# Rounding the second token group in place, its last view at the turn from self to cross tiles, and other lists for the front

## The chip, the cores and the metric

The program runs on one core of one Trainium2 chip, in one launch. The metric is the device time of that launch in microseconds (us). A profiled execution also gives the start and length of each instruction on each engine: PE (TensorE), DVE (VectorE), ACT (ScalarE), POOL (GpSimd) and SP, which here only issues DMAs.

## What is computed

A block of two decoder layers over 1024 tokens of 256 channels (16 batches of 64 tokens, `ctx_2048` having the same shape). The reference, cut to what matters here:

```python
x = x + tanh(g_xattn[0]) * L0_attention(layernorm(x), mask, ctx, ctx, Wq, bq, Wk, bk, Wv, bv)
x = x + tanh(g_ffn[0])   * L0_ffn(layernorm(x))       # ternary weights, 8-bit tokens
x = x + tanh(g_xattn[1]) * L1_attention(layernorm(x), ctx)
x = x + tanh(g_ffn[1])   * L1_experts(layernorm(x))   # shared + 7 routed, top 3

def L0_ffn(x):                       # bit_linear rounds x to 8 bits and w to -1, 0, 1
    h = silu(bit_linear(x, w_gate)) * bit_linear(x, w_up)
    return bit_linear(rms_norm(h, ln_weight), w_down)

def L1_attention(hidden, cond):      # 16 query heads, 8 key heads of 128
    ln_out = ln(hidden) * ln_w + ln_b
    q, k, v = (fp8(ln_out / in_scale[m]) * in_scale[m] @ w[m].T * w_scale[m] for m in "qkv")
    core = gqa(ln(q), ln(k), v)                        # self part
    qx = fp8(ln_out / qx_in_scale) ...                 # fourth view of ln_out
    kx, vx = split(cond @ w_kv_x.T)
    xout = gqa(ln(qx), ln(kx), vx)                     # cross part
    return fp8(concat(core, xout) / smooth) @ wproj.T * scale
```

So the normed tokens are rounded to fp8 four times, once for each "view" (q, k, v, qx), each with its own input scale.

## The kernel before, in words

**Two programs one behind the other.** `front` computes the first layer (attention and the ternary feed-forward layer), the products of the context with `w_kv_x` (24 of 32 units, `context(e)`) and the splitting of the first weights of the second layer into a high and a low part. `grouped_attention` computes the second layer: 16 tiles of 128 tokens, of which tiles 0 to 7 are the self part and tiles 8 to 15 the cross part, and behind them the experts.

**Order.** Each engine has a list of calls that is written out by hand; an engine takes its calls strictly in that order, and semaphores make a call wait for others. SP's list sets the order of the loads. The tokens are worked on in two groups s = 0, 1 of four 128-row pieces. In `front` the calls that matter here are: `weights.mean / centre / high / low (n)`, the mean over heads on DVE, its subtraction on POOL (L185), the high part on ACT (L195) and the low part on DVE (L202) of weight block n; `context_mean / centre_context`, the same for the context weights; `tern.column_sum / scale / clip`, the rounding of the three ternary weights on ACT (L580, L594) and DVE (L600, L602); `gate_up`, `gated`, `hidden(s, n)` (L1280, L1057, L863), the products, the SiLU and the 16 products of the two halves of the gated layer; `square`, `weigh`, `hidden_largest`, `hidden_scales`, `round_hidden` (L889), the norm and 8-bit rounding of `f_h`; `turn_hidden` (L1294), `keep_hidden` (L1072) and `down` (L1306), its transposes and the last product; `turn_normed`, `weigh_tokens` (L1332, L1085), the normed tokens of the second layer.

**The fp8 rounding.** It has a division by the scale on ACT (`over_scale`, L2039 for the second token group) and five instructions on DVE: clip, exponent bits, power, add, subtract (L1797 to L1809). Group 0 of the tokens is rounded in `front` by `round_two`. Group 1 is tokens 512 to 1023, which tiles 4 to 7 (views 0 to 2) and 12 to 15 (view 3) use; it is rounded in `grouped_attention`, in `late_tokens(view)`, through the buffers `yb` and `kb` with two halves each. So `over_scale` of view v waits for `late_tokens(v - 2)`, and `unload(0, ...)`, which writes `yb` next, waits for all four. The calls stand in DVE's list so: `late_tokens(0)` and `(1)` in `ahead(0)`, `(2)` and `(3)` at the start of `both_own(0)`, ahead of `less_max(0, 0)` (L1742, L1746), the maximum that scores and exponents of tile 0 go through.

**Tiles.** `both_own(n)` works on tile n's attention and on the projections of tile n + 1; `both_cross(n)` does the same from n = 7 on, where tile n + 1 is a cross tile. `copy_tile(n)` on POOL (L1607) takes a tile's views out of `xq`; `fp8(n, h)` on POOL (L1632, `g_cat`) is the last step of the rounding of a tile's attention; `own_out.low` (L231) the low part of the output weights.

## Time and profile before

| | before |
|---|---|
| median of 3 runs | 638.5 us (638.17 to 638.55) |
| profiled execution, its own time | 637.83 us |
| its span, first to last instruction | 636.1 us |
| mean granted clock of PE | 0.976 of full speed |
| busy share of the span, from the page | PE 92%, DVE 78%, ACT 58%, POOL 58% |
| `front`, to about | 145.1 us |
| first scores of tile 0 turned into exponents | 183.8 us |
| end of the self tiles, about | 331 us |

The profiled execution is 1.7 us longer than its span and 0.7 us shorter than the median. An engine's busy share says little by itself; what matters in each stretch is which engine is never idle, and what the others wait for.

### The profile page before, as it was taken

Reading aid. Unit: us, or ns where it says so; the run is one execution under the profiler, and the core shown is the slowest. Engines: PE = TensorE matmul, PEld = TensorE weight load, DVE = VectorE, ACT = ScalarE, POOL = GpSimd, SP = SyncE. Lnnn points to the kernel's source line nnn. Section 1 sums busy time; section 2 is a strip of 40 time slices with the busy share of each in tenths; the row PEclk is TensorE's granted clock in tenths of the full one; section 3 lists DMA queues with packets and bytes.
Section 4 is the critical chain, followed back from the end, with each engine's and each line's share of the span. In section 5 each row is a group of like instructions: output and inputs, shape, how many; then the busy total and the mean of one; then the engine's idle time right before and its main releaser. Section 6 shows DMA issues by size and latency. Waiting matters only on the chain.

```text
span 636.1 us, 10615 instructions
## 1 busy us (share of the span) xinstructions
PE 582.5 (92%) x3738; PEld 471.0 (74%) x3738; DVE 496.7 (78%) x924; ACT 370.2 (58%) x669; POOL 366.1 (58%) x299
## 2 busy tenths in 40 slices
PE   3999786978869999999998999999999999999996
PEld 1655333644558898888987898888889888888886
DVE  4488999886998999998979889999987956333333
ACT  1477675485666676776767765676666235434231
POOL 3100765303656878778778866766766733855431
PEclk9999898998969999999999999999999999999999
DMA  7981220114413112131085132322110100311001
GB/s 236 294 305 66 84 82 33 68 66 152 144 39 133 36 60 73 35 124 43 2 312 174 46 116 67 85 83 80 49 57 18 34 1 2 112 39 33 2 1 66
DMA packets 44564, 54.86 MB, mean 86 GB/s; under 512 B 8417, under 2 KB 30817, under 8 KB 44513
## 3 DMA queue, kind: packets, MB, share of 16 engines
q1 hardware_dynamic: 44512, 54.20, 26.1%
q8 instruction: 30, 0.49, 0.3%
q14 instruction: 22, 0.17, 0.1%
HBM read 41.60 MB, written 12.58 MB: 85 GB/s over the span
## 4 chain that ended last, share of the span: by engine, by line
PE 62%; DVE 5%; POOL 4%; ACT 3%; issue 2%; DMA 1%; DVEq 0%; POOLq 0%; ACTq 0%
PE g_proj L2220 12%; PE g_proj L2306 7%; PE g_scores L2261 6%; PE g_turn L2250 6%; PE g_op L2287 5%; PE g_op L474 2%; PE g_op L476 2%; PE g_op L475 2%; PE g_proj L459 2%; PE g_proj L461 2%; PE g_proj L460 2%; PE g_turn L2270 2%; POOL g_rs L1613 1%; PE g_turn L459 1%; PE g_scores L459 1%
## 5 line engine op out<-in xcount | busy, mean ns | idle before, releaser
L1613 POOL TENSOR_TENSOR g_rs<-g_ve,neg_half 128x4 f32<-128x4 f32 x80 | 83.5, 1048 | 37.8 <-DVE g_ve L1723 37.4
L1632 POOL TENSOR_TENSOR g_cat<-g_yb,g_kb 128x1024 fp32r<-128x1024 bf16 x32 | 71.0, 2226 | 41.1 <-DVE g_yb L1780 41.1
L2220 PE MATMUL g_proj<-w_hi,g_xqc 128*128 128x512 f32 x192 | 85.1, 443 | 1.5 <-DVE g_qn L1736 1.2
L2220 PE MATMUL g_proj<-w_lo,g_xqc 128*128 128x512 f32 x192 | 77.2, 402 | 0.0
L503 POOL TENSOR_TENSOR m_h_lo<-m_h,m_h_hi 128x512 fp32r<-128x512 f32 x32 | 41.4, 1296 | 57.1 <-ACT m_h_hi L490 57.1
L1723 DVE TENSOR_REDUCE g_ve<-g_sq 128x4 f32<-128x516 f32 x80 | 54.6, 684 | 18.4 <-ACT g_sq L1980 16.8
L2261 PEld LDWEIGHTS g_scores<-g_qkT 128*128 128x128 f32 x512 | 62.4, 196 | 8.1 <-issue 6.9
L2261 PE MATMUL g_scores<-g_qkT 128*128 128x64 f32 x512 | 62.8, 277 | 4.8 <-DVE g_ex L1746 4.8
L2250 PE MATMUL g_turn<-ident,g_qn 128*128 128x128 f32 x384 | 58.0, 278 | 1.3 <-DVE g_qn L1736 1.3
L1980 ACT ACTIVATE g_sq<-g_proj 128x512 f32<-128x512 f32 x80 | 47.7, 596 | 16.3 <-PE g_proj L2220 14.5
L2250 PEld LDWEIGHTS g_turn<-ident,g_qn 128*128 128x128 f32 x384 | 45.0, 143 | 10.8 <-DVE g_qn L1736 2.6
L1323 PE MATMUL f_bank<-f_w_ctx,f_ctxT 128*128 128x512 f32 x96 | 47.1, 622 | 1.8 <-ACT f_kept L1079 1.1
L490 ACT ACTIVATE m_h_hi<-m_h 128x512 fp32r<-128x512 f32 x32 | 20.2, 632 | 48.6 <-DVE m_h L497 48.6
L2220 PEld LDWEIGHTS g_proj<-w_hi,g_xqc 128*128 128x128 f32 x192 | 37.3, 194 | 10.2 <-DVE g_qn L1736 2.1
L2014 ACT ACTIVATE g_qkT<-g_turn,c_lnp 128x512 f32<-128x512 f32 x48 | 36.5, 777 | 14.2 <-PE g_turn L2250 14.2
L1736 DVE TENSOR_TENSOR g_qn<-g_proj,g_rs 128x512 f32<-128x512 f32 x64 | 43.7, 682 | 1.3 <-POOL g_rs L1613 1.3
L2287 PE MATMUL g_op<-g_pT,g_v 64*128 64x128 f32 x512 | 37.2, 285 | 5.5 <-ACT g_pT L2033 5.5
L513 DVE SCALAR_TENSOR_TENSOR x_res<-g_op,m_we,x_res 128x256 f32<-128x256 f32 x64 | 27.8, 478 | 17.8 <-PE g_op L476 17.8
L2287 PEld LDWEIGHTS g_op<-g_pT,g_v 64*128 64x128 f32 x512 | 31.1, 187 | 14.4 <-ACT g_pT L2033 10.0
L2220 PEld LDWEIGHTS g_proj<-w_lo,g_xqc 128*128 128x128 f32 x192 | 37.4, 195 | 5.5 <-issue 0.8
L555 POOL TENSOR_TENSOR ln_rstd<-ln_ve,neg_half 128x4 f32<-128x4 f32 x6 | 6.6, 1094 | 58.3 <-DVE ln_ve L542 58.3
L2014 ACT ACTIVATE g_qkT<-g_turn,x_lnp 128x512 f32<-128x512 f32 x48 | 36.2, 771 | 5.6 <-PE g_turn L2250 5.6
(247 smaller groups left out, 1662.4 us busy)
## 6 DMA issues: line engine op xcount, KB each, us to landing
kvx_rows<-f_kept SPq DMA_DIRECT2D x24, 256.0 KB, 2.4
g_ksq<-kvx_rows SPq DMA_DIRECT2D x8, 512.0 KB, 4.4
g_kraw<-kvx_rows SPq DMA_DIRECT2D x16, 256.0 KB, 3.2
g_v<-kvx_rows SPq DMA_DIRECT2D x8, 512.0 KB, 4.0
m_raw<-in_L_W SPq DMA_DIRECT2D x16, 256.0 KB, 3.0
c_raw<-in_L_wqT SPq DMA_DIRECT2D x4, 512.0 KB, 5.8
f_w_ctx<-in_L_wkvxT SPq DMA_DIRECT2D x4, 512.0 KB, 8.1
c_praw<-in_L_wprojT SPq DMA_DIRECT2D x4, 512.0 KB, 5.4
```

The lines of the kernel that those rows point to most:

```text
L1323: last = T.matmul(context_bank(e)[:], ctxT[:, c_, tile * P:(tile + 1) * P], w_ctx[:, chunk, c_, :], start=c_ == 0, stop=c_ == KT - 1)
L1613: G.tensor_tensor(rs[:, at % NORMS, :], ve[:, at % NORMS, :], k["half"][:, 0:4], ALU.pow).then_inc(q["rs_done"], 1)
L1632: G.tensor_tensor(cat[:, h].rearrange("p h (b s) -> p b h s", b=2), yb[:, h, :].rearrange("p (b h s) -> p b h s", b=2, s=SEQ), kb[:, h, :] ...
L1723: V.tensor_reduce(ve[:, at % NORMS, :], sq[:, at % 2], AX.X, ALU.add).then_inc(q["ve_done"], 1)
L1736: V.tensor_tensor(qn[:, i % 2, :].rearrange("p (h d) -> p h d", d=D), bank(n, i)[:].rearrange("p (h d) -> p h d", d=D), bcast(rs[:, at % N ...
L1980: A.activation(sq[:, at % 2, :, 0:D], bank(n, i)[:].rearrange("p (h d) -> p h d", d=D), ACT.Square, scale=D ** -0.5).then_inc(q["sq_done"], 1)
L2014: A.activation(qkT[:, n % 2, at:at + 4, :], turns[TURN_BANK[i]][:].rearrange("p (h m) -> p h m", h=4), ACT.Identity, bias=lnp[:, w + 1:w + ...
L2220: last = T.matmul(bank(n, i)[:], xqc[:, n % 2, view * KT + c_, :], w[:, c_, :], start=c_ == 0 and part == 0, stop=c_ == KT - 1 and part == 1)
L2250: last = T.transpose(out, qn[:, i % 2, h * D:(h + 1) * D], k["ident"][:])
L2261: last = T.matmul(sp_[:, (g * 2 + b) * SEQ:(g * 2 + b + 1) * SEQ], qkT[:, n % 2, 2 * kv + b, :], qkT[:, n % 2, HEADS + kv, rows], start=Tr ...
L2287: last = T.matmul(op[:, b, g * P:(g + 1) * P], v[rows, n % 2, kv * D:(kv + 1) * D], pT[rows, h, g, :], start=True, stop=True)
L2306: last = T.matmul(proj[OUT_BANK][:, 0:E], cat[:, h, hd % (2 * GH), :], w[hd // 4][:, hd % 4, :], start=hd == 0 and part == 0, stop=hd == H ...
```

## The change

Four things are done.

1. **In place.** `over_scale` writes the divided tokens straight to `xq`, for every view, and waits for no rounding. `late_tokens` rounds them there (`round_tokens`, which `early_tokens` shares), with `kb[:, 0]` alone as its second buffer. The five instructions of a view are the same.
2. **Where the views are rounded.** `late_tokens(2)` stands behind `less_max(0, 0)` and the two `sums` of tile 1; `late_tokens(3)` stands in `both_cross(7)`, behind `less_max(7, 0)`, and waits there for `fp8(6, 0)` on POOL (`cat_done`).
3. **Waits.** `copy_tile(4)` waits for three views, `copy_tile(12)` for the fourth; `unload(0, ...)` waits for none; `fp8(0, ...)` waits for the last `over_scale`.
4. **Other lists in `front`**, on all five engines. No call is added or removed; the one reciprocal `inv` and all others only move.

The diff, cut to its core (of the lists, the first lines on SP; what the others do is shown in the orders below):

```diff
@@ SP, front @@
             sp.dma_start(k['x'][:, 0:ST, :], source[:, 0:ST, :]).then_inc(x_loaded[0], 16)
-            sp.dma_start(k['x'][:, ST:TILES, :], source[:, ST:TILES, :]).then_inc(x_loaded[1], 16)
+            weights.load(sp, t, 0)
+            weights.load(sp, t, 1)
+            sp.dma_start(mask[:], t['mask'].rearrange('(n p) s -> p n s', p=P)).then_inc(q['v_loaded'], 16)
...
+            weights.load(sp, t, 2)
+            sp.dma_start(k['x'][:, ST:TILES, :], source[:, ST:TILES, :]).then_inc(x_loaded[1], 16)
@@ POOL, grouped_attention @@
                     if n == ST:
-                        pool.wait_ge(q["late_done"], 4)
+                        pool.wait_ge(q["late_done"], 3)
...
+                    if n == TILES + ST:
+                        pool.wait_ge(q["late_done"], 4)
@@ DVE, grouped_attention @@
                 def unload(n, h):
                     dve.wait_ge(q["pv_done"], n * 2 + h + 1)
-                    if n == 0:
-                        dve.wait_ge(q["late_done"], 4)
...
+                def round_tokens(view, group, name):
+                    y, power_ = k["xq"][:, view, :, group * ST * P:(group + 1) * ST * P], kb[:, 0, :].rearrange("p (c n) -> p c n", c=KT)
+                    done = view + 1 if group else 1
+                    V.tensor_scalar(y, y, FP8_MAX, -FP8_MAX, ALU.min, ALU.max).then_inc(q[name + "_clipped"], 1)
+                    dve.wait_ge(q[name + "_clipped"], done)
+                    V.tensor_scalar(power_.bitcast(U16), y.bitcast(U16), 0x7F80, None, ALU.bitwise_and).then_inc(q[name + "_abs"], 1)
+                    dve.wait_ge(q[name + "_abs"], done)
+                    V.tensor_scalar(power_, power_, FP8_NORMAL, FP8_LIFT, ALU.max, ALU.mult).then_inc(q[name + "_power"], 1)
+                    dve.wait_ge(q[name + "_power"], done)
+                    V.tensor_tensor(y, y, power_, ALU.add).then_inc(q[name + "_big"], 1)
+                    dve.wait_ge(q[name + "_big"], done)
+                    V.tensor_tensor(y, y, power_, ALU.subtract).then_inc(q[name + "_done"], 1)
...
+                def late_tokens(view, n=0):
+                    if n > 0:
+                        dve.wait_ge(q["cat_done"], 2 * n - 1)
                     dve.wait_ge(q["over_done"], KT * (view + 1))
...
                 def both_own(n):
                     m = n + 1
-                    if n == 0:
-                        late_tokens(2)
-                    if n == 0:
-                        late_tokens(3)
                     less_max(n, 0)
                     sums(m, 0)
                     sums(m, 1)
+                    if n == 0:
+                        late_tokens(2)
                     total(n, 0)
...
                     less_max(n, 0)
+                    if n == TILES - 1:
+                        late_tokens(3, n)
                     sums(m, 1)
@@ ACT, grouped_attention @@
                 def over_scale(u):
                     view = u // KT
-                    if view > 1:
-                        act.wait_ge(q["late_done"], view - 1)
-                    A.activation(yb[:, view % 2, u % KT * CH:(u % KT + 1) * CH], k["late"][:, u % KT, :], ACT.Copy, scale=k["inv"][:, u:u + 1]).then_inc(q["over_done"], 1)
+                    A.activation(k["xq"][:, view, u % KT, ST * P:TOK], k["late"][:, u % KT, :], ACT.Copy, scale=k["inv"][:, u:u + 1]).then_inc(q["over_done"], 1)
```

**ACT in `front`, from the exponents of group 1 to the first SiLU.** Before (`f_probs` is `exponent`, `f_pT` `keep_probs`, `f_raw` `tern.scale`, `w_hi` `weights.high`, `f_kept` `keep_context`, `f_xqT` `keep_integers`, `f_silu` `gated`):

```order
L594 ACTIVATE f_raw_85<-f_raw_85,magic,tern_inverse 128x2048
L1037 ACTIVATE f_probs<-f_s 64x4x64 x2
L1041 ACTIVATE f_pT<-f_bank 128x512
L594 ACTIVATE f_raw_86<-f_raw_86,magic,tern_inverse 128x2048
L1079 ACTIVATE f_kept<-f_bank 128x512 x2
L1048 ACTIVATE f_xqT<-f_bank,unmagic 128x512 x2
L1079 ACTIVATE f_kept<-f_bank 128x512
L1057 ACT_TABLE_LOAD
L1057 ACTIVATE f_silu<-f_bank,f_dg 128x512
```

and now:

```order
L1037 ACTIVATE f_probs<-f_s 64x4x64 x2
L1041 ACTIVATE f_pT<-f_bank 128x512
L594 ACTIVATE f_raw_85<-f_raw_85,magic,tern_inverse 128x2048
L195 ACTIVATE w_hi<-c_raw_50,c_sc 128x512 x2
L1079 ACTIVATE f_kept<-f_bank 128x512
L594 ACTIVATE f_raw_86<-f_raw_86,magic,tern_inverse 128x2048
L1079 ACTIVATE f_kept<-f_bank 128x512
L1048 ACTIVATE f_xqT<-f_bank,unmagic 128x512 x2
L1079 ACTIVATE f_kept<-f_bank 128x512 x2
L195 ACTIVATE w_hi<-c_raw_51,c_sc 128x512 x2
L1057 ACT_TABLE_LOAD
L1057 ACTIVATE f_silu<-f_bank,f_dg 128x512
```

The first `tern.scale` stood ahead of the exponents and stands behind the transposed probabilities; two `weights.high` and one `keep_context` came in ahead of the first SiLU.

**PE in `front`, from the last products of the gated layer to the first `down`.** Before (L1280 is `gate_up`, L1323 `context`, L1294 `turn_hidden`, L1306 `down`):

```order
L1323 MATMUL f_bank<-f_w_ctx,f_ctxT 128x512 x4
L1280 MATMUL f_bank<-f_values,f_xqT 128x512 x8
L1294 MATMUL f_bank<-ident,f_h 128x128 x16
L1323 MATMUL f_bank<-f_w_ctx,f_ctxT 128x512 x2
L1294 MATMUL f_bank<-ident,f_h 128x128 x8
L1306 MATMUL f_bank<-f_values,f_hT 128x256 x16
L1323 MATMUL f_bank<-f_w_ctx,f_ctxT 128x512 x2
```

and now:

```order
L1280 MATMUL f_bank<-f_values,f_xqT 128x512 x4
L1323 MATMUL f_bank<-f_w_ctx,f_ctxT 128x512 x2
L1280 MATMUL f_bank<-f_values,f_xqT 128x512 x4
L1323 MATMUL f_bank<-f_w_ctx,f_ctxT 128x512 x4
L1294 MATMUL f_bank<-ident,f_h 128x128 x8
L1323 MATMUL f_bank<-f_w_ctx,f_ctxT 128x512 x4
L1294 MATMUL f_bank<-ident,f_h 128x128 x8
L1306 MATMUL f_bank<-f_values,f_hT 128x256 x8
L1323 MATMUL f_bank<-f_w_ctx,f_ctxT 128x512 x2
```

`context(14)` and `context(15)` stood ahead of the last two `gate_up` and are behind them. The second `turn_hidden` waits now behind `context(16)` and `context(17)`, which wait for the last `hidden`. On DVE the low parts of weight blocks 2, 3 and 4 stand ahead of that last `hidden` (before: of blocks 2 and 3), and `hidden_largest(1, 0)` behind it (before: well ahead of it). Farther up in DVE's list the means of blocks 2 and 3 and the first context mean, which stood between the products of `hidden`, are ahead of `hidden(0, 0)`.

**DVE in `grouped_attention`, tile 0.** Before, the five instructions of a view's rounding stand twice behind `scale(0, 5)` (L1736), and behind the second five `less_max(0, 0)` and the rest (L1797 to L1809 are the second five, L1742 and L1746 `less_max`, L1723 `sums`, L1752 and L1756 `total`):

```order
L1797 TENSOR_SCALAR g_yb<-g_yb 128x1024
L1803 TENSOR_SCALAR g_kb<-g_yb 128x1024
L1805 TENSOR_SCALAR g_kb<-g_kb 128x1024
L1807 TENSOR_TENSOR g_yb<-g_yb,g_kb 128x1024
L1809 TENSOR_TENSOR xq_all<-g_yb,g_kb 128x2x512
L1742 TENSOR_REDUCE g_mx<-g_scores 128x8
L1746 TENSOR_TENSOR g_ex<-g_scores,g_mx 128x512
L1723 TENSOR_REDUCE g_ve<-g_sq 128x4 x2
L1752 TENSOR_REDUCE g_sm<-g_ex 128x8
L1756 RECIPROCAL g_rc<-g_sm 128x8
L202 SCALAR_TENSOR_TENSOR w_lo<-x_raw_57,x_sc,w_hi 128x512 x2
```

and now, from `scale(0, 5)` on (L1787 to L1795 are the rounding of the one view that stayed):

```order
L1740 TENSOR_TENSOR g_qn<-g_proj,g_rs 128x512
L1746 TENSOR_REDUCE g_mx<-g_scores 128x8
L1750 TENSOR_TENSOR g_ex<-g_scores,g_mx 128x512
L1727 TENSOR_REDUCE g_ve<-g_sq 128x4 x2
L1787 TENSOR_SCALAR xq_all<-xq_all 128x2x512
L1789 TENSOR_SCALAR g_kb<-xq_all 128x1024
L1791 TENSOR_SCALAR g_kb<-g_kb 128x1024
L1793 TENSOR_TENSOR xq_all<-xq_all,g_kb 128x2x512
L1795 TENSOR_TENSOR xq_all<-xq_all,g_kb 128x2x512
L1756 TENSOR_REDUCE g_sm<-g_ex 128x8
L1760 RECIPROCAL g_rc<-g_sm 128x8
L202 SCALAR_TENSOR_TENSOR w_lo<-x_raw_57,x_sc,w_hi 128x512 x2
```

`less_max(0, 0)` and two sums of tile 1 are ahead of the rounding. The other view stands where the cross tiles begin, where `sums(8, 1)` (L1727) used to follow on `less_max(7, 0)` at once:

```order
L1778 TENSOR_SCALAR g_kb<-g_kb 128x1024
L1782 TENSOR_TENSOR g_yb<-g_yb,g_kb 128x1024 x2
L1746 TENSOR_REDUCE g_mx<-g_scores 128x8
L1750 TENSOR_TENSOR g_ex<-g_scores,g_mx 128x512
L1787 TENSOR_SCALAR xq_all<-xq_all 128x2x512
L1789 TENSOR_SCALAR g_kb<-xq_all 128x1024
L1791 TENSOR_SCALAR g_kb<-g_kb 128x1024
L1793 TENSOR_TENSOR xq_all<-xq_all,g_kb 128x2x512
L1795 TENSOR_TENSOR xq_all<-xq_all,g_kb 128x2x512
L1727 TENSOR_REDUCE g_ve<-g_sq 128x4
L1756 TENSOR_REDUCE g_sm<-g_ex 128x8
L1760 RECIPROCAL g_rc<-g_sm 128x8
```

## Rows read from the trace of the kernel before

**Rows 1.** Windows: us, busy (count) by engine, granted clock, DMA share, GB/s

```profile
57.70:104.00 46.30, 38.28 (x122) 16.21 (x120) 45.47 (x59) 32.67 (x55) 27.28 (x13) 0.96 0.18 69
104.00:108.00 4.00, 0.40 (x2) 0.40 (x3) 4.00 (x5) 1.40 (x3) 1.01 (x1) 0.91 0.16 59
108.00:135.00 27.00, 26.25 (x153) 18.27 (x152) 22.58 (x51) 17.55 (x30) 7.25 (x4) 0.95 0.13 50
179.00:184.00 5.00, 0.19 (x2) 0.16 (x1) 4.93 (x5) 0.84 (x2) 2.80 (x1) 0.84 0.00 0
184.00:188.00 4.00, 3.88 (x17) 3.69 (x18) 3.47 (x7) 4.00 (x9) 3.53 (x4) 0.50 0.00 0
199.00:320.00 121.00, 120.07 (x919) 105.76 (x916) 112.33 (x185) 84.22 (x160) 92.75 (x72) 1.00 0.17 55
```

**Rows 2.** Timeline of PE in tile 0: start, length, instruction [idle before]

```profile
183.88 3.65 PE L2261 MATMUL g_scores<-g_qkT 128*128 128x64 f32 x16 [4.81 <-DVE g_ex L1746]
...
187.64 0.80 PE L2220 MATMUL g_proj<-w_hi,g_xqc 128*128 128x512 f32 x1
...
191.07 0.78 PE L2220 MATMUL g_proj<-w_hi,g_xqc 128*128 128x512 f32 x1
```

**Rows 3.** Timeline of ACT in the front

```profile
46.59 2.09 ACT L594 ACTIVATE f_raw<-f_raw,magic,tern_inverse 128x2048 f32<-128x2048 f32 x1
...
56.90 0.69 ACT L1057 ACTIVATE f_silu<-f_bank,f_dg 128x512 f32<-128x512 f32 x1
```

**Rows 4.** Timeline of DVE at the first and the thirteenth product of the gated layer

```profile
57.69 0.75 DVE L863 SCALAR_TENSOR_TENSOR f_h<-f_bank,f_du,f_silu 128x512 f32<-128x512 f32 x1 [1.77 <-ACT f_silu L1057]
...
99.42 1.41 DVE L863 SCALAR_TENSOR_TENSOR f_h<-f_bank,f_du,f_silu 128x512 f32<-128x512 f32 x2
```

**Rows 5.** Groups of DVE by shape, 57.69 to 108.2 us | busy, mean ns | idle

```profile
L202 DVE SCALAR_TENSOR_TENSOR w_lo<-c_raw,c_sc,w_hi 128x512 fp32r<-128x512 f32 x6 | 6.3, 1092 | 0.0
...
L178 DVE TENSOR_REDUCE c_sums<-c_raw 128x8 f32<-128x1024 f32 x4 | 4.8, 1206 | 0.0
...
L180 DVE TENSOR_SCALAR c_sums<-c_sums 128x8 f32<-128x8 f32 x4 | 3.9, 970 | 0.1
...
L602 DVE TENSOR_SCALAR f_values<-f_values 128x2048 bf16<-128x2048 bf16 x1 | 2.7, 2728 | 0.0
...
L879 DVE TENSOR_SCALAR f_hm<-f_hm 128x4 f32<-128x4 f32 x1 | 2.3, 2287 | 0.0
```

**Rows 6.** Timeline of DVE, end of tile 0's late rounding

```profile
174.88 0.42 DVE L1797 TENSOR_SCALAR g_yb<-g_yb 128x1024 bf16<-128x1024 bf16 x1
...
176.98 0.69 DVE L1809 TENSOR_TENSOR xq_all<-g_yb,g_kb 128x1024 bf16<-128x1024 bf16 x1
...
179.69 2.71 DVE L1809 TENSOR_TENSOR xq_all<-g_yb,g_kb 128x1024 bf16<-128x1024 bf16 x1
...
182.33 0.68 DVE L1742 TENSOR_REDUCE g_mx<-g_scores 128x8 f32<-128x512 f32 x1
```

**Rows 7.** Timeline of POOL beside it

```profile
179.06 2.80 POOL L231 TENSOR_TENSOR p_lo<-c_praw,p_hi 128x1024 fp32r<-128x1024 f32 x1 [6.11 <-ACT p_hi L227]
```

**Rows 8.** Timeline of PE from the second transpose of f_h on

```profile
107.60 1.97 PE L1294 MATMUL f_bank<-ident,f_h 128*128 128x128 f32 x8 [3.64 <-DVE f_h L889]
...
132.64 2.13 PE L1306 MATMUL f_bank<-f_values,f_hT 128*128 128x256 bf16 x16
```

**Rows 9.** Groups of PE by shape, 107.6 to 134.8 us

```profile
L1323 PE MATMUL f_bank<-f_w_ctx,f_ctxT 128*128 128x512 f32 x25 | 12.6, 622 | 0.0
...
L1294 PE MATMUL f_bank<-ident,f_h 128*128 128x128 f32 x56 | 8.2, 296 | 4.3 <-DVE f_h L889 4.3
...
L1306 PE MATMUL f_bank<-f_values,f_hT 128*128 128x256 bf16 x64 | 8.0, 273 | 0.0
```

**Rows 10.** Timeline of DVE at the change from self to cross tiles

```profile
334.94 0.69 DVE L1723 TENSOR_REDUCE g_ve<-g_sq 128x4 f32<-128x516 f32 x1 [3.33 <-ACT g_sq L1980]
```

**Rows 11.** Timeline of POOL at the same place

```profile
329.38 4.62 POOL L1632 TENSOR_TENSOR g_cat<-g_yb,g_kb 128x1024 fp32r<-128x1024 bf16 x2 [2.63 <-DVE g_yb L1780]
```

More of the change, by code:

```diff
@@ L1120, in _ @@
             keep_context(2)
+            keep_context(3)
+            weights.high(act, 2)
             gated(0, 0)
@@ L1400, in _ @@
             turn_normed(0)
[L1401 removed]
             turn_hidden(1, 2)
+            down(1, 1)
             context(21)
[L1404 removed]
+            context(22)
             turn_hidden(1, 3)
```

253 lines of the change are left out of this document (114 added, 139 removed).

## The prediction

> **What bounds the kernel now.** I read the page's busy shares first: PE 92%, DVE 78%. They are averages over three kinds of stretch, so I went to windows. From 199 to 320 us (tiles 1 to 6) PE is busy 120.07 of 121.00 us at full clock [rows 1]: whatever is gained ahead of it is carried through it, and nothing that DVE does there is on the path. In the front from 57.7 to 104 us DVE is busy 45.47 of 46.30 us and PE only 38.28, so DVE's list sets the pace; from 108 to 135 us it is PE, 26.25 of 27.00 us, behind a hole in which it worked 0.40 of 4.00 us [rows 1]. In tile 0 PE is busy 0.19 us of the 5 us from 179 to 184 while DVE is busy 4.93 of them [rows 1]: PE waits 4.81 us for `g_ex` [rows 2]. These three places, and the turn to the cross tiles, are what the change touches.
>
> **Front, the start: 3.2 us later.** Before, ACT has scaled the first ternary matrix when it keeps the transposed probabilities of group 1, and scales the second directly behind them, at 46.59 [rows 3]. Now the first stands behind those probabilities too. The second transpose of tokens (1.0 us by `turn`'s eight matmuls) now stands ahead of `project_v(0)`, so I put the probabilities 1.1 us later, at 47.7. From there ACT has 2.09 + 2.09 us of scaling [rows 3], one `weights.high` (some 1.3) and one `keep_context` (0.6) between them: 54.5 where it was 48.7. Behind it DVE clips (some 1.9), and ACT, beside that, keeps integers and contexts, one more `weights.high`, then loads the SiLU table (1.3). I come to the first SiLU at 60.2 where it is 56.90 [rows 3], and to the first `hidden` at 60.9 where it is 57.69 [rows 4]: +3.2.
>
> **Front, what DVE has done by then.** Two weight means and a context mean came ahead of `hidden(0, 0)`, into time in which DVE waits. One mean is 1.21 us and a small instruction [rows 5], 1.33 in all, so three are 4.0 us. Net, DVE is 4.0 - 3.2 = 0.8 us ahead.
>
> **Front, DVE against POOL.** The small second instruction of a mean should take 0.17 us, but over four it means 0.97; a low part is six instructions of mean 1.09 where those without POOL beside them take 0.74, and single ones take 2.73 and 2.29 us [rows 5] for some 0.7 and 0.2. They run long where a big POOL operation is under way: in tile 0 a subtract of 0.69 us takes 2.71 [rows 6] from 179.69 on, until just behind the end of POOL's 2.80 us from 179.06 [rows 7]. To the end of `hidden(1, 5)` such excess is some 11.3 us: means 3.2 (4 x 0.80), the clip 2.0, the scales 2.1 + 1.1, two more small ones 1.3 and 1.6. I walked the new lists from 60.9 on with these lengths, each such instruction held until POOL's is done, and counted 9.7, since two of POOL's centrings are out of the stretch: -1.6. Against that two low parts more (1.3 each) and one `hidden_largest` less (1.1) stand ahead of that product, +1.5. It comes at about 100.1 to 100.5 us, against 99.42 + 1.41 = 100.8 [rows 4]: no gain yet.
>
> **Front, the end: -1.8 us.** Here the order on PE decides. Before, PE waits 3.64 us for the second rounded row until 107.60 [rows 8], and works at a granted 0.91 and then 0.95 [rows 1]. Now `context(14)` and `(15)` fill that hole, behind `gate_up(1, 7)` at 101.4: transposes from 104.9, then `context(16)` to 107.4, when the last `hidden` (104.5) is long there. What remains from there to the last `down` is what remained at 107.60: seven transposes of eight, six contexts, eight `down`, one `turn_normed`. At full clock these are 6.1 + 10.3 + 7.0 + 0.9 = 24.3 us; it took 27.2 (132.64 + 2.13 = 134.77) [rows 8], with contexts at a mean of 622 ns and transposes at 296, and the eight `down` 8.0 us in all [rows 9]. About 1.5 of the 2.9 us between is the clock behind the hole, which goes if the hole goes: the last `down` at 133.0, -1.8, and the tail behind it (norm, roundings) is unchanged. The loads are in another order; the one that is moved back furthest and needed soonest is the context, which comes near the end of the queue now. No engine waited for it before, its first product moves 3 us back as well, and by 57.7 the queue is all but empty (a share of 0.18) [rows 1]: I put nothing on them.
>
> **Tile 0: -2.2 us.** One view's rounding on DVE costs 2.79 us where nothing disturbs it (174.88 to 176.98 + 0.69) [rows 6]. `less_max(0, 0)` starts at 182.33 [rows 6] behind two of them and POOL's lock; now it starts when `scale(0, 5)` is done, 174.9. So `scores(0, 1)` goes from 183.88 [rows 2] to behind `project(1, 1)`, 178.9. That is 5.0 us, but not all of it arrives. Next late is ACT, whose exponents of tile 0, a split and an output weight precede `scale(1, 0)`: 184.0, and `project(1, 2)` with it, against 187.64 [rows 2]. And next the view that stayed: it waits for `own_out.low(0)` on POOL (which ends at 181.8, as before [rows 7]) and ends at 184.6, then total, low part, `less_max(0, 1)`, and `scale(1, 1)` ends at 188.7. `project(1, 3)` starts there, against 191.07 [rows 2]: -2.4. I take 0.2 off for a low part behind POOL's normalising. PE has a granted 0.50, its lower level of 1.2 GHz, from 184 to 188 [rows 1]; that should shrink, but it lies beside DVE's chain.
>
> The Trainium skill (TensorE: Matmul & The Clock Gate, HAM oscillation) says that waits between bursts keep the engine falling back to half its clock. By that rule a wait of 3 us that remains ahead of `project(1, 2)` would leave the bursts slow, and the sum would be nearer to nothing from this tile. The trace agrees that waits and half clock lie together here (0.19 of 5 us busy, then 0.50, [rows 1]).
>
> **The view that went: +1.9 us.** Behind `less_max(7, 0)` DVE is idle for 3.33 us, until 334.94 [rows 10], and the rounding takes 2.79. It would fit, if it started at once (331.6). But its clip waits for `fp8(6, 0)`, the first of two `g_cat` operations that take 4.62 us from 329.38 [rows 11]; when that is done, POOL goes on with the second, to 334.0, and DVE's clip is of the kind that runs long under POOL. Then the five end at 336.8, and `sums(8, 1)` is 1.9 us late. DVE is full from there on (the chain of waits goes through it to 352), so it is carried. The bounds: 0, if the clip gets in ahead of POOL, and 2.8, if POOL's next work is pushed too.
>
> The Trainium skill (SBUF — State Buffer, Who interferes with whom) says that whichever of a two-port DVE instruction and a GpSimd instruction starts first holds the port pair for its whole length, and the other blocks. By it the clip loses to the second `g_cat`, +1.9; by the idle row alone it would be 0.
>
> **The sum.** -1.8 - 2.2 + 1.9 = -2.1 us. The profiled execution has 637.83 us, so 635.7; the median is 0.7 above it: **636.4 us**. About 0.2% (1.3 us) can be told from no change.
>
> **Rivals.**
> - *Slower: the late start is not caught up.* POOL's operations fall on DVE's instructions as often as before (+1.6 on my walk), and DVE waits for SiLUs between products, since ACT has its high parts there; 2.5 us more for that. Then the front is +2.3, the sum +2.0: about 640.5. It decides from a `hidden(1, 5)` later than some 102.5 us. For it: ACT is behind by 3.2 us and the three means are small. Against: ACT has slack, 32.67 of 46.30 us busy [rows 1]. Chance 0.18.
> - *Tile 0 brings nothing:* by half clock or by ACT's and POOL's queues. Then -1.8 + 1.9: 638.6. For it: PE's 0.50 [rows 1]. Against: 5 us of wait are there to take. Chance 0.15.
> - *The front's end brings nothing,* since transposes wait for `keep_hidden` and the rest balances: 638.2. Chance 0.14.
> - *The moved view is hidden* in the idle 3.33 us [rows 10]: 634.5. Chance 0.13.
>
> **How the numbers follow.** The forecast, 636.4, has 0.40; its own range is 635.0 to 637.8, from half to all of each gain. Low end: the hidden view, and a little more from tile 0, 633.6. High end 640.0, just short of the slower rival; about 0.1 lies above it and 0.07 below 633.6. Faster by over 1.3 us: 0.13, and 0.36 of the forecast's 0.40, and 0.05 of the others: 0.54. Same: 0.26. Slower: 0.20, the slower rival and a little of the next.
>
> **What would show it.** The first `hidden` near 60.9 and the last near 104.5; PE without a hole of 3 us between 101 and 110; `front` ending near 143.3. From the start of tile 0 to `project(1, 3)` 2.4 us less. At the turn, a clip (now L1787) of over 2 us and `sums(8, 1)` late. The forecast is wrong if the first SiLU is late by more than 5 us, if the last `hidden` is behind 108, or if that clip is short.

## The result, and the profile after

The change makes the kernel faster: 634.0 us (median of 14 runs, 632.95 to 637.1) against 638.2 us (14 runs, 637.53 to 639.01), a ratio of 0.9941 with a 95% interval of 0.993 to 0.9951, so 3.8 us (0.59%) less; between the two medians it is 4.2. The profiled execution has 633.74 us, its span 632.0 us, 4.1 less than before. The forecast was 636.4 with a range of 633.6 to 640.0: the measured time lies near the low end of that range, and outside of the forecast's own range of 635.0 to 637.8. One of the 11 executions of e3 below (1165.1 us), and one of the kernel before beside e9 to e11 (831.49), fell in a slower state and are left out of the ratios.

Busy shares barely move. These are the lines of the page on the engines and on the clock that the throttle granted:

```profile
PE 576.7 (91%) x3735; PEld 468.2 (74%) x3738; DVE 494.6 (78%) x924; ACT 369.1 (58%) x669; POOL 365.9 (58%) x299
...
PEclk9999999988989999999998999999999999999999
```

The windows that answer to [rows 1], each at about the place where that work stands now (columns as there):

```profile
59.10:102.00 42.90, 32.43 (x104) 13.31 (x105) 41.81 (x58) 29.09 (x49) 22.62 (x12) 1.00 0.16 62
102.00:106.00 4.00, 4.00 (x17) 2.23 (x16) 4.00 (x5) 2.48 (x6) 4.00 (x2) 1.00 0.35 131
104.00:131.00 27.00, 26.10 (x156) 17.94 (x155) 21.78 (x49) 18.77 (x32) 7.22 (x5) 1.00 0.16 59
175.00:180.00 5.00, 1.12 (x11) 0.98 (x9) 4.12 (x7) 4.46 (x10) 4.48 (x3) 1.00 0.00 2
180.00:184.00 4.00, 3.70 (x12) 2.57 (x12) 3.93 (x7) 1.08 (x2) 2.72 (x3) 0.57 0.00 0
195.00:316.00 121.00, 120.12 (x922) 105.58 (x921) 112.30 (x185) 84.35 (x161) 92.96 (x72) 1.00 0.18 60
...
333.00:337.00 4.00, 3.68 (x20) 3.68 (x21) 3.21 (x5) 2.73 (x4) 4.00 (x5) 0.63 0.21 75
```

The 4 us in which PE worked 0.40 us are full now, and the tail of the front has a granted 1.00. In tile 0 PE still waits, and still works at its lower level behind the wait. A new window at the lower level (0.63) is there at the turn to the cross tiles.

**Front.** DVE's first and last product of the gated layer, then PE from the last products of that layer on, and its last `down`:

```profile
59.09 0.75 DVE L863 SCALAR_TENSOR_TENSOR f_h<-f_bank,f_du,f_silu 128x512 f32<-128x512 f32 x1 [2.57 <-ACT f_silu L1057]
...
97.36 0.74 DVE L863 SCALAR_TENSOR_TENSOR f_h<-f_bank,f_du,f_silu 128x512 f32<-128x512 f32 x1
...
101.33 0.74 DVE L863 SCALAR_TENSOR_TENSOR f_h<-f_bank,f_du,f_silu 128x512 f32<-128x512 f32 x1
```

```profile
98.16 1.04 PE L1280 MATMUL f_bank<-f_values,f_xqT 128*128 128x512 bf16 x4
99.03 3.60 PE L1323 MATMUL f_bank<-f_w_ctx,f_ctxT 128*128 128x512 f32 x8
102.47 1.04 PE L1294 MATMUL f_bank<-ident,f_h 128*128 128x128 f32 x8
103.34 3.60 PE L1323 MATMUL f_bank<-f_w_ctx,f_ctxT 128*128 128x512 f32 x8
...
128.72 2.13 PE L1306 MATMUL f_bank<-f_values,f_hT 128*128 128x256 bf16 x16
```

Against [rows 4] the first `hidden` is 1.4 us later, `hidden(1, 5)` ends 2.7 us earlier (98.1 for 100.8), and against [rows 8] the last `down` ends at 130.85, 3.9 us earlier.

**Tile 0.** PE at the three products that the prediction follows ([rows 2]), then DVE's maximum and the view that stayed, and POOL beside it ([rows 6, 7]):

```profile
174.23 1.89 PE L2258 MATMUL g_scores<-g_qkT 128*128 128x64 f32 x16
180.19 0.63 PE L2217 MATMUL g_proj<-w_hi,g_xqc 128*128 128x512 f32 x1 [4.07 <-ACT g_qn L2005]
...
185.25 0.50 PE L2217 MATMUL g_proj<-w_hi,g_xqc 128*128 128x512 f32 x1 [1.36 <-DVE g_qn L1740]
```

```profile
171.75 0.68 DVE L1746 TENSOR_REDUCE g_mx<-g_scores 128x8 f32<-128x512 f32 x1
...
176.41 1.59 DVE L1787 TENSOR_SCALAR xq_all<-xq_all 128x1024 bf16<-128x1024 bf16 x1
...
175.36 2.36 POOL L231 TENSOR_TENSOR p_lo<-c_praw,p_hi 128x1024 fp32r<-128x1024 f32 x1 [5.54 <-ACT p_hi L227]
```

`project(1, 3)` comes at 185.25 for 191.07, 5.8 us earlier: 1.9 more than the front gave. By the second output of attention of that tile (192.05 for 198.23) it is 2.3 us.

**The turn.** DVE's view and the sums behind it, POOL beside it, and PE ([rows 10, 11]); the last two lines are PE at this place before:

```profile
325.77 2.36 DVE L1787 TENSOR_SCALAR xq_all<-xq_all 128x1024 bf16<-128x1024 bf16 x1 [0.31 <-POOL g_cat L1636]
328.16 0.43 DVE L1789 TENSOR_SCALAR g_kb<-xq_all 128x1024 uint16<-128x1024 uint16 x1
...
330.43 0.68 DVE L1727 TENSOR_REDUCE g_ve<-g_sq 128x4 f32<-128x516 f32 x1
...
331.25 1.01 POOL L1615 TENSOR_TENSOR g_rs<-g_ve,neg_half 128x4 f32<-128x4 f32 x1 [3.41 <-DVE g_ve L1727]
...
333.32 0.66 PE L2267 MATMUL g_turn<-ident,g_ex 128*128 128x128 f32 x4 [3.19 <-POOL g_ex L1625]
333.73 0.36 PE L2303 MATMUL g_proj<-p_hi,g_cat 128*128 128x256 f32 x1
...
334.08 0.41 PE L2303 MATMUL g_proj<-p_hi,g_cat 128*128 128x256 f32 x1
```

```profile
337.85 0.66 PE L2270 MATMUL g_turn<-ident,g_ex 128*128 128x128 f32 x4 [1.57 <-POOL g_ex L1623]
...
338.46 0.28 PE L2306 MATMUL g_proj<-p_lo,g_cat 128*128 128x256 f32 x1
```

The clip of 0.43 us takes 2.36, the sums come at 330.43 where 334.94 less the 6.15 us gained until then would be 328.79: 1.6 us late. PE waits 3.19 us where it waited 1.57, and then products of 0.28 us take 0.41. The granted clock of the 4 us from the end of the wait is 0.59 (333.3 to 337.3), before it was 1.00 (337.85 to 341.85).

**A table by stretches.** The executions begin this work up to 1.6 us apart, so I count from ACT's last copy of keys (L1031; 39.02 before, 38.90 after). Some loads, means and other calls ahead of it are in another order too; to that mark they make 0.12 us. Stretches in us: from there to the end of the last `down` (front); to the second output of attention on PE in tile 0; to that in tile 6; to that in tile 9 (the turn, tiles 7 to 9); and on to tile 15. Differences of start times read from PE's timeline:

| kernel | front | tile 0 | tiles 1 to 6 | turn | rest | median us | ratio to before, 95% |
|---|---|---|---|---|---|---|---|
| before | 95.75 | 63.46 | 126.17 | 58.71 | 111.12 | 638.2 | |
| the change | 91.95 | 61.20 | 126.20 | 60.74 | 111.19 | 634.01 | 0.993 to 0.9951 |
| e1_tiles_alone | 97.18 | 60.98 | 126.19 | 60.73 | 111.15 | 638.48 | 0.9998 to 1.0015 |
| e2_lists_alone | 91.97 | 63.86 | 126.21 | 59.20 | 111.10 | 634.35 | 0.9922 to 0.9949 |
| e3_view_back | 91.98 | 66.19 | 126.28 | 59.13 | 111.19 | 638.05 | 0.9981 to 0.9999 |
| e4_view_tile4 | 93.56 | 60.92 | 129.75 | 58.71 | 111.27 | 636.43 | 0.9958 to 0.9982 |
| e5_scale_early | 91.97 | 61.14 | 126.19 | 60.72 | 111.27 | 635.01 | 0.9928 to 0.9952 |
| e6_means_late | 96.15 | 61.23 | 126.25 | 60.79 | 111.11 | 640.16 | 1.001 to 1.0034 |
| e7_halves_own | 91.98 | 61.06 | 127.61 | 59.26 | 111.27 | 634.73 | 0.9928 to 0.9951 |
| e8_halves_cross | 91.94 | 61.53 | 126.30 | 69.45 | 111.22 | 642.98 | 1.005 to 1.0074 |
| e9_scales_early | 91.96 | 61.60 | 126.40 | 60.74 | 111.28 | 635.3 | 0.9936 to 0.996 |
| e10_contexts_back | 94.46 | 61.43 | 126.35 | 60.75 | 111.24 | 637.45 | 0.9974 to 1.0006 |
| e11_half_half | 91.95 | 61.05 | 127.48 | 59.58 | 111.24 | 634.31 | 0.993 to 0.9958 |
| e12_silu_first | 91.43 | 62.13 | 126.21 | 61.44 | 111.27 | 634.64 | 0.9922 to 0.9954 |

The change against before: -3.80 - 2.26 + 0.03 + 2.03 + 0.07, and -0.12 of start, are the 4.05 us between the two last outputs (490.18 and 494.23). One profiled execution stands behind each row, and single ones stray (the front of e4 has 93.56, where eight others with the same lists on DVE and PE have 91.94 to 91.98; that of e1 has 97.18 with the lists of before).

### The profile page after: what moved, and what is told of

Its sections match the earlier page's. It is cut to its first block, busy times and chain, and to the rows that moved or that the text cites. A ratio compares the mean times of both kernels' runs of the same rounds, so it can differ in the third digit from the quotient of the medians.

```text
span 632.0 us, 10614 instructions
## 1 busy us (share of the span) xinstructions
PE 576.7 (91%) x3735; PEld 468.2 (74%) x3738; DVE 494.6 (78%) x924; ACT 369.1 (58%) x669; POOL 365.9 (58%) x299
## 4 chain that ended last, share of the span: by engine, by line
PE 64%; DVE 6%; POOL 3%; issue 3%; ACT 2%; DVEq 0%; POOLq 0%; ACTq 0%
PE g_proj L2217 13%; PE g_proj L2303 8%; PE g_scores L2258 7%; PE g_turn L2247 6%; PE g_op L2284 5%; PE g_op L474 3%; PE g_op L475 2%; PE g_op L476 2%; PE g_proj L459 2%; PE g_proj L461 2%; PE g_proj L460 2%; PE g_turn L2267 2%; PE g_op L2225 1%; POOL g_rs L1615 1%; PE g_turn L459 1%
## 5 line engine op out<-in xcount | busy, mean ns | idle before, releaser
L1727 DVE TENSOR_REDUCE g_ve<-g_sq 128x4 f32<-128x516 f32 x80 | 54.8, 685 | 16.9 <-ACT g_sq L1979 14.9
L2258 PEld LDWEIGHTS g_scores<-g_qkT 128*128 128x128 f32 x512 | 60.9, 192 | 2.7 <-issue 1.4
L2258 PE MATMUL g_scores<-g_qkT 128*128 128x64 f32 x512 | 61.0, 272 | 0.0
L1323 PE MATMUL f_bank<-f_w_ctx,f_ctxT 128*128 128x512 f32 x96 | 44.0, 594 | 0.9 <-ACT f_kept L1079 0.9
```

What stands on the lines that cost most here:

```text
L1323: last = T.matmul(context_bank(e)[:], ctxT[:, c_, tile * P:(tile + 1) * P], w_ctx[:, chunk, c_, :], start=c_ == 0, stop=c_ == KT - 1)
L1727: V.tensor_reduce(ve[:, at % NORMS, :], sq[:, at % 2], AX.X, ALU.add).then_inc(q["ve_done"], 1)
L2258: last = T.matmul(sp_[:, (g * 2 + b) * SEQ:(g * 2 + b + 1) * SEQ], qkT[:, n % 2, 2 * kv + b, :], qkT[:, n % 2, HEADS + kv, rows], start=Tr ...
```

## The experiments

Kernels of e1 to e4, of e5 to e8 and of e9 to e11 ran on one chip each, e12 on a fourth. The kernel before has a median of 638.17, 638.59, 638.40 and 638.38 us on these chips, and of 638.2 where it ran beside the change; so a comparison with the change's 634.01 is uncertain by some 0.4 us on top of the spread of each kernel.

**e1: the tiles' edits without the lists.** `front` of before, `grouped_attention` of the change.

> The lists of the front as before; in-place rounding and the two moved views as in the change. Theory 1 (the gain of the whole, about 4.1 us, is the front's 3.9 and tile 0's 2.3 less the turn's 2.05, and these add up): about 0.25 us less than before, ratio 0.9996 to the kernel before, no difference that can be told, the first scores of tile 0 some 5 us earlier and the second output of attention (PE, end of tile 0) 2.3 us earlier than before. Rival (tile 0 can only give its gain when the front's end is as in the change, since half clock or the queues of ACT and POOL hold it): tile 0 gives under 1 us and the kernel is 1 to 2 us slower than before, ratio 1.002 to 1.003.

Measured 638.48, ratio 1.0007: no difference. The profile has the two parts as the theory had them: tile 0 is 2.5 us shorter (60.98 for 63.46) and the turn 2.0 longer. They cancel. The rival, that tile 0 needs the new front for its gain, falls.

**e2: the lists alone.** `front` of the change, `grouped_attention` of before.

> The kernel before with the new lists of the front alone; all views rounded in tile 0, through the buffers. Theory 1: the front ends 3.9 us earlier and all of it arrives: 3.9 us less than before, ratio 0.9939. Rival (the whole change's gain is mostly the moved views, and an earlier front is partly waited away in tile 0): under 2.5 us less, ratio above 0.996.

Measured 634.35, ratio 0.9935: all of the gain is here. The profile's front is 91.97, as with the whole change.

**e3: the fourth view back in tile 0.**

```diff
                     if n == 0:
                         late_tokens(2)
+                        late_tokens(3)
...
                     less_max(n, 0)
-                    if n == TILES - 1:
-                        late_tokens(3, n)
                     sums(m, 1)
```

> As the change, but the fourth view of the second group is rounded directly behind the third in tile 0 again, behind the first maximum and the two sums; nothing at the turn. Theory 1: the turn gives its 2.05 us back, tile 0 loses 2.3 to 2.8 (the total and the second maximum of tile 0 stand behind one more rounding of 2.8 us, and the next product of the projections waits for the scaling behind them): 0.2 to 0.8 us slower than the change. Rival (the gain of tile 0 comes from the maximum standing ahead of both roundings, and the second rounding there is free since PE waits for ACT anyway): 1.5 to 2 us faster than the change.

Measured 638.05, 4.0 us slower than the change and far outside of what both theories said. The turn gives 1.6 us back, but tile 0 loses 5.0 (66.19 for 61.20). PE in tile 0:

```profile
179.53 0.69 PE L2216 MATMUL g_proj<-w_hi,g_xqc 128*128 128x512 f32 x1 [4.07 <-ACT g_qn L2004]
...
185.02 0.66 PE L2266 MATMUL g_turn<-ident,g_ex 128*128 128x128 f32 x4 [2.67 <-POOL g_ex L1625]
187.49 0.80 PE L2216 MATMUL g_proj<-w_hi,g_xqc 128*128 128x512 f32 x1 [1.81 <-DVE g_qn L1740]
188.09 0.63 PE L2216 MATMUL g_proj<-w_lo,g_xqc 128*128 128x512 f32 x1
```

Two waits follow on the first one, and products of 0.40 us go on taking 0.63 until 192, where those of the change are back at 0.40 by 185.6. Of the 5.0 us, 3.1 are more waiting (2.67 + 1.81 against the change's 1.36), the rest is slow products. So with the maximum ahead of it, only one view has room in tile 0. At the turn, PE's wait is back at 1.56 us, and still its clock falls behind it (shown in the part on the turn below); in e4, where it doesn't, 2.0 us come back.

**e4: the fourth view in tile 4** and not at the turn, behind `total(4, 1)`, where PE is never idle.

```diff
                     total(n, 1)
+                    if n == 4:
+                        late_tokens(3, n)
                     sums(m, 3)
```

> As the change, but the fourth view is rounded in tile 4, behind the second total, where PE is the bound (120.07 of 121 us busy before) and DVE has some 1.4 us of idle time in each tile. Theory 1 (DVE is off the path there and catches up over two tiles): the turn's 2.05 us come back and nothing is lost: 2.0 us faster than the change, and no wait of PE over 0.5 us between 240 and 300 us. Rival (DVE's list feeds PE just in time, so 2.8 us less the nearest idle time are carried): PE waits about 2 us in tile 4 or 5, and the kernel is within 0.8 us of the change.

Measured 636.43, 2.4 us slower than the change. The turn gives its 2.0 us back; tiles 1 to 6 take 3.55 us more. PE behind the rounding, whose five instructions took 2.7 us undisturbed:

```profile
277.65 0.66 PE L2247 MATMUL g_turn<-ident,g_qn 128*128 128x128 f32 x4 [1.90 <-DVE g_qn L1740]
278.06 0.68 PE L2217 MATMUL g_proj<-w_hi,g_xqc 128*128 128x512 f32 x1
278.54 0.63 PE L2217 MATMUL g_proj<-w_lo,g_xqc 128*128 128x512 f32 x1
...
281.79 0.39 PE L2217 MATMUL g_proj<-w_lo,g_xqc 128*128 128x512 f32 x1
```

```profile
278.00:282.00 4.00, 4.00 (x15) 3.07 (x13) 3.80 (x7) 2.83 (x7) 3.74 (x4) 0.57 0.38 116
```

A wait of 1.90 us, and then 4 us at a granted 0.57; 3.55 less 1.90 leaves 1.65 us to the slow products. The profiled execution (637.72 us) is the slowest of the eight; that the clock falls in each of them isn't shown. The prediction's reading of that stretch as one in which nothing that DVE does is on the path was wrong: DVE feeds PE just in time there.

**e5, e9: what sets the first SiLU.** e5 moves ACT's first scaling ahead of the exponents again, e9 the second too.

```diff
+            tern.scale(act, 0)
             exponent(1)
             keep_probs(1)
-            tern.scale(act, 0)
+            tern.scale(act, 1)
             weights.high(act, 1)
             keep_context(0)
-            tern.scale(act, 1)
```

(This is e9; e5 has the first two of the four marked lines.)

> As the change, but ACT scales the first ternary matrix ahead of the exponents of group 1 again, where it is idle for 4.17 us. Theory 1 (the first SiLU is set by ACT's chain behind the transposed probabilities, and the front goes on from it): the 2.09 us come out of that chain, the first hidden comes about 2.0 us earlier (57.1), and since DVE is full from there on and PE from the end of the front, the kernel is 1.5 to 2.0 us faster than the change. Rival (the first SiLU then waits for something else, the context products or the table, or DVE's instructions meet POOL's at worse moments): under 0.5 us of gain, or a loss.

> As the change, but ACT scales both ternary matrices early: the first ahead of the exponents of group 1, the second directly behind the transposed probabilities, ahead of the high part and the first kept context. With the first alone early the first SiLU did not come earlier, since ACT then waited 2.44 us for the first context product of PE at 49.70. Theory 1 (the second scaling, 2.08 us, goes into that wait, and the chain from the first kept context to the SiLU gets shorter by it): the first SiLU about 2.0 us earlier, the last hidden and the kernel 1.5 to 2.0 us earlier than the change. Rival (PE's next products or DVE's rounding of the matrices take over): the first SiLU less than 0.7 us earlier and the time within 0.7 us of the change.

Measured 635.01 and 635.3, no better than the change. From the mark to the first `hidden` it is 20.19 us in the change, 20.19 in e5 and 20.19 in e9. Both scalings are hidden. In e9 ACT waits for PE's contexts instead:

```profile
52.58 0.60 ACT L1079 ACTIVATE f_kept<-f_bank 128x512 f32<-128x512 f32 x1 [1.12 <-PE f_bank L1323]
...
56.02 0.60 ACT L1079 ACTIVATE f_kept<-f_bank 128x512 f32<-128x512 f32 x1 [1.12 <-PE f_bank L1323]
56.51 1.32 ACT L195 ACTIVATE w_hi<-c_raw,c_sc 128x512 fp32r<-128x512 f32 x2
57.85 1.28 ACT L1057 ACT_TABLE_LOAD   x1
```

**e12: the first SiLU sooner.**

```diff
             context(2)
-            context(3)
             gate_up(0, 0)
+            context(3)
...
             keep_context(2)
-            keep_context(3)
-            weights.high(act, 2)
             gated(0, 0)
+            keep_context(3)
             tern.scale(act, 2)
             gated(0, 1)
+            weights.high(act, 2)
```

> As the change, but context(3) stands behind gate_up(0, 0) on PE, and on ACT its keeping and the high part of block 2 stand behind the first SiLU. Theory (after two runs in which both scalings came early and the first SiLU did not: what sets it is PE's run of four context products, 7.03 us, and the high part of 1.3 us behind the last of them): the first product of the gated layer ends near 55.5, the table load stands at 55.6, the first SiLU at 56.9 instead of 58.3, the first hidden 1.4 us earlier; with DVE full from there on, the kernel is 0.8 to 1.4 us faster than the change. Rival (the time of the front after the first hidden isn't DVE's alone, or its instructions meet POOL's at other moments): the first hidden 1.4 us earlier, but less than half of it in the last hidden and in the kernel's time.

The first `hidden` stands 18.97 us behind the mark, 1.2 earlier: the fourth context product and the high part are what set it. But the last one comes 62.41 us behind the mark, for 62.43: the rival is right. By `hidden(0, 4)` some half of it is lost (29.83 for 30.37 us), to a wait of 1.47 us for the fourth SiLU, behind the high part; the other half goes in a low part of block 3 that takes 2.54 us for 2.03. The front ends 0.5 us earlier; in the profiled execution tile 0 takes 0.9 us more and the turn 0.7 more than in the change, the turn with a granted 0.50 behind its wait of 3.21 us. By the median (634.64) it can't be told from the change.

**e6: two of the three means back among the products.**

```diff
-            weights.mean(dve, 3)
             ln.apply(dve, 2, lambda j: xn[:, 0, j, :])
             largest(0)
-            context_mean(0)
...
             hidden(0, 7)
+            context_mean(0)
             hidden(1, 0)
```

(The mean of block 3 stands where that of 4 did, that of 4 behind `round_tokens(1)`. POOL's list is edited too: its centrings of block 3 and of the first context weights go back to where the kernel before had them, two and three of POOL's norm operations (L750) later.)

> As the change, but the mean of weight block 3 and the first context mean stand between the products of the gated layer again (of blocks 3 and 4 the first is done there as well), with POOL's centrings where they were. Theory 1 (the front's gain is DVE time that moved ahead of the first hidden): 2.66 us more of DVE behind the first hidden, the last hidden 2.7 us later or somewhat more with POOL's operations in the way, and the kernel 2.0 to 3.0 us slower than the change. Rival (the gain comes from PE's order at the end, and DVE's part is covered by it): under 1 us slower.

Measured 640.16, 6.2 us slower than the change; the profiled front is 4.2 longer. 2.7 us of DVE moved back, with POOL's two centrings, cost 4.7 at the last `hidden` (67.14 us behind the mark for 62.43), since other instructions now fall on POOL's. How much of it is the new place of the centrings was not tested apart. The costliest, and POOL beside it:

```profile
82.04 5.17 DVE L202 SCALAR_TENSOR_TENSOR w_lo<-c_raw,c_sc,w_hi 128x512 fp32r<-128x512 f32 x2
...
82.00 2.36 POOL L750 TENSOR_TENSOR f_h<-f_h,f_lnw 128x1024 f32<-128x1024 f32 x1 [8.31 <-ACT f_junk L1064]
84.31 2.35 POOL L185 TENSOR_TENSOR c_raw<-c_raw,c_sums 128x1024 f32<-128x1024 f32 x1
```

A low part, two instructions that take 1.41 us where nothing disturbs them, takes 5.17, until 0.55 us behind the end of POOL's second operation (86.66).

**e10: contexts back ahead of the last two products.**

```diff
-            gate_up(1, 6)
             context(13)
+            context(14)
+            gate_up(1, 6)
+            context(15)
             gate_up(1, 7)
-            context(14)
-            context(15)
```

(ACT's list is changed to match.)

> As the change, but on PE context(13) and (14) stand ahead of gate_up(1, 6) and context(15) ahead of gate_up(1, 7), nearer to the order of before, with ACT's list to match. Theory 1 (the filled hole counts): gate_up(1, 6) comes 3.4 us and gate_up(1, 7) 1.7 us later, the last hidden some 1.9 us later, PE waits for it ahead of context(16) by 0.5 to 2 us, and the last down comes 1 to 2.5 us later; the kernel 1 to 2.5 us slower than the change. Rival (DVE sets the end, PE's order doesn't matter): within 0.5 us of the change.

Measured 637.45, 3.4 us slower than the change (its 12 executions spread from 635.96 to 641.50); by the profile the front is 2.5 longer. DVE waits 1.87 us for a SiLU, the last `hidden` comes 2.0 later, and PE waits again:

```profile
103.59 3.67 PE L1323 MATMUL f_bank<-f_w_ctx,f_ctxT 128*128 128x512 f32 x8 [0.85 <-DVE f_h L863]
```

**e7, e8, e11: the fourth view in halves.** Each half is 512 columns, with a power buffer in tokens that are no longer needed (view 0 of tokens 0 to 511), so that it waits for nothing of POOL. The whole view at the turn is gone in all three.

```diff
+                def late_half(c_, n):
+                    y, power_ = k["xq"][:, 3, c_, ST * P:TOK], k["xq"][:, 0, c_, 0:ST * P]
...
                     total(n, 1)
+                    if n in (3, 5):
+                        late_half((3, 5).index(n), n)
```

(e7. In e8 the halves stand ahead of `less_max(8, 0)` and `less_max(9, 0)`; in e11 one behind `total(4, 1)`, one behind `less_max(7, 0)`.)

> As the change, but the fourth view is rounded in two halves of 512 columns, in tiles 3 and 5 behind the second total, with a power buffer of its own in tokens that are no longer needed, so that it doesn't wait for POOL's last step. Each half is about 1.5 us of DVE. Theory 1 (a stretch of DVE longer than its idle time there makes PE wait, and when PE waits 1.9 us its clock falls to the lower level for some 3 us and costs 1.6 more, as the whole view did in tile 4: 3.5 us): each half makes PE wait some 0.5 us and the clock stays up, so 1.0 us for both, and the kernel is about 1.0 us faster than the change. Rival (the cost is proportional: no matter how it is cut, 3.5 us): the kernel is 1.5 us slower than the change, as with the whole view in tile 4.

> As the run before it, but the halves stand in tiles 8 and 9, ahead of the first maximum, where DVE waits 0.68 and 1.03 us for scores. Theory 1: each half is late by 0.5 to 0.8 us at first, PE has 0.7 us of idle time of its own in each of these tiles, so 0.5 to 1.0 us for both: about 1.0 to 1.5 us faster than the change. Rival (PE's idle time there is behind DVE's chain, and the first products wait for more): no faster than the change.

> As the change, but the fourth view is rounded in two halves with the power buffer of their own, one in tile 4 behind the second total, one at the turn behind the first maximum of tile 7. Theory 1: the half in tile 4 costs 0.69 us, as each did in tiles 3 and 5; the one at the turn starts 0.3 us earlier, its first two-port instruction still ends with POOL's second g_cat, and the sums come 0.5 to 0.9 us later than without it, so PE's wait stays below 2.5 us: 0.5 us faster than the change. Rival (the wait behind POOL at the turn costs the same for a half as for the whole): 0.3 to 0.7 us slower than the change.

e7: 634.73. In tiles 3 and 5 PE waits 0.42 us each and keeps its clock:

```profile
252.49 0.66 PE L2262 MATMUL g_turn<-ident,g_qn 128*128 128x128 f32 x4 [0.42 <-DVE g_qn L1740]
252.90 0.48 PE L2232 MATMUL g_proj<-w_hi,g_xqc 128*128 128x512 f32 x1
253.21 0.40 PE L2232 MATMUL g_proj<-w_lo,g_xqc 128*128 128x512 f32 x1
```

Tiles 1 to 6 take 1.4 us more, where the whole view cost 3.55: the same work in two parts costs less than half. The turn gives 1.5 back and not e4's 2.0, as its products behind a wait of 1.69 us take 0.42:

```profile
332.70 0.66 PE L2282 MATMUL g_turn<-ident,g_ex 128*128 128x128 f32 x4 [1.69 <-POOL g_ex L1625]
...
333.34 0.42 PE L2318 MATMUL g_proj<-p_lo,g_cat 128*128 128x256 f32 x1
```

So nothing is left of it in the median; the expected 1.0 us did not come.

e11: 634.31, and one half in tile 4 costs 1.3 (PE waits 0.92 us there), the half at the turn still makes PE wait 1.98 us, with products of 0.41 us behind it. e8 is 9 us slower than the change, beyond both theories:

```profile
347.87 0.29 DVE L1802 TENSOR_SCALAR xq_all<-xq_all 128x512 bf16<-128x512 bf16 x1
348.19 2.14 DVE L1804 TENSOR_SCALAR xq_all<-xq_all 128x512 uint16<-128x512 uint16 x1
...
353.05 3.65 PE L2273 MATMUL g_scores<-g_qkT 128*128 128x64 f32 x16 [2.74 <-DVE g_ex L1750]
```

An instruction of 0.3 us meets POOL's `g_cat` (348.03 to 350.18) and takes 2.14; the maximum is late, PE waits 2.74 us, and its scores take 3.65 us for 1.9. Tile 9 does the same (2.13, 1.74, 3.44). The turn's stretch is 8.7 us longer.

No version here beats the change by more than can be told.

## Why the prediction was right, and where it was not

**Tile 0, -2.2: measured -2.3.** The order was as followed: the maximum no longer waits for two roundings, next late is ACT (PE waits 4.07 us for its scaling), next the view that stayed and what is behind it. e1 shows it without the new front: -2.5. With the front's 3.9 us added, to stand beside the forecast on the axis of before: the maximum 175.7 (174.9 forecast), the second scores 178.1 (178.9), `project(1, 2)` 184.1 (184.0), `project(1, 3)` 189.2 (188.7).

**The turn, +1.9: measured 1.6 at the sums and +2.0 in tile 9.** The clip lost to POOL's second `g_cat`, as followed, 2.36 us for 0.43. What the prediction lacked is the clock: at the first output of attention of tile 7 (338.69 for 341.69) only 3.0 of the 6.15 us gained until then are left. 1.6 of the 3.15 lost are there when PE's wait ends (333.32 for 337.85), the other 1.5 are products at the lower level. Of the 3.15, 1.3 us come back by tile 8 (3.68 us ahead at the second output of tile 7, 4.32 at that of tile 8, then 4.12 at that of tile 9): before, PE waited 0.45 and 0.43 us there for a `g_ex` that POOL makes behind two low parts of 4.7 us in all, and now it comes to it later and doesn't wait. So the 2.0 us are 1.6 of DVE's delay and some 0.4 of the clock, and that they meet the forecast's 1.9 so well is in part luck.

The clock isn't the moved view's alone either. In e3 and e2 the turn has no fourth view, PE waits 1.56 and 1.60 us, and the clock falls to 0.57 and 0.59 of full speed in the 4 us from there; before and in e4 it waits 1.57 us and keeps 1.00. From e3:

```profile
336.35 0.85 PE L2266 MATMUL g_turn<-ident,g_ex 128*128 128x128 f32 x4 [1.56 <-POOL g_ex L1625]
...
337.22 0.41 PE L2302 MATMUL g_proj<-p_lo,g_cat 128*128 128x256 f32 x1
```

The turn's stretch is 58.71 us where the clock stays up (before, e4) and 59.13 to 59.26 where it falls (e2, e3, e7): 0.4 to 0.5 us. The Trainium skill (TensorE: Matmul & The Clock Gate, HAM oscillation) has a kernel with waits between its bursts keep falling back to the lower clock. The traces agree that the fall comes behind waits (0.41 us for 0.28), but not behind each of them, and equal waits end both ways; what decides it stays open.

**The front, -1.8: measured -3.8 to -3.9.** This is the term that was mis-sized, and all of the difference to the forecast. Of its steps:

- *The start, +3.2:* it was +1.4 (1.5 from the mark). Of the 1.8 us between, 1.5 are the probabilities, which I had at 47.7 and which end at 46.2. The step that failed is the 1.1 us for the second transposes of tokens: they stood ahead of `project_v(0)` before, too, and only changed places with `scores(0)`. The other 0.4 are most likely a low part, which went from ahead of DVE's maximum of group 1 (40.96 before) to behind it (47.02); that is read from the lists, not tested. From the probabilities to the first SiLU I had 12.5 us and it is 12.1 (46.2 to 58.3), but by a wrong chain: I named ACT's two scalings, and e5 and e9 take both out of the way and nothing moves, while e12 moves a context product and a high part and gains 1.2. That the length came out is luck. (Its parts as written, 2.09 + 2.09 + 1.3 + 0.6 from 47.7 on, also make 53.8 and not the 54.5 that I went on from.)
- *DVE from there to `hidden(1, 5)`:* I had three means done (4.0), 1.6 less of waiting for POOL, 1.5 more work, so 4.1 us less; measured, to the start of the next instruction, 38.9 us (59.09 to 98.02) against 43.05 (57.69 to 100.74), 4.1 less. The terms were right, but their sum from 60.9 on is 99.9, and I wrote 100.1 to 100.5. The lengths of DVE's instructions beside POOL's came out right as a sum (1.38 + 0.45 for two small instructions of means, 2.75 for two product scales, 2.1 + 0.46 + 0.62 for three low parts, 1.57 for a mean square: 9.3 us, where I counted 9.7), though not one by one. e6 bears on the means' part: without two of them, and with POOL's centrings back, 4.7 us are lost.
- *The end:* the filled hole holds (e10: 2.5 us by the profile), and so does the length from the end of context(16) to the last `down`: 25.6 us forecast, 25.8 measured (105.06 to 130.85). It only began 2.3 us earlier: `gate_up(1, 7)` is done at 99.0, where I had 101.4. That is the 1.8 us of the start (59.09 for 60.9) and 0.6 on DVE's way from there, of which 0.2 to 0.6 is the slip in the sum.

So the start's error reaches the result by this argument: 1.8 us at the first SiLU, carried by a full DVE and then a full PE. No run tests it, and e12 warns against it as a rule: 1.2 us more at the same place did not arrive. Nor was the order of the loads, which changed too, tested apart from the other lists.

**The sum.** -1.8 - 2.2 + 1.9 = -2.1 forecast, -3.8 - 2.3 + 2.0 = -4.1 measured in the profiled executions. By the medians the tiles' two terms are nothing together (e1) and the lists are the whole gain (e2). In the profiles with the new front the tiles' edits gain some 1.1 (2.66 in tile 0 less 1.54 at the turn), the medians of e2 and the change differ by 0.3 with intervals that overlap: how much of it is there stays open.

**The rivals.** The late start was caught up, so the slow case falls; tile 0 and the front's end both brought their gain, so the two middle ones fall as well; the moved view was not hidden (e4 and e7 show what that would be worth, 2.0 and 1.5 us of the turn).
